# An FFN inside a fused attention block: its steps in twos instead of one by one

## What is computed

```
gate_logits = xf @ Wg + bg
top_w, top_i = jax.lax.top_k(gate_logits, TOP_K)
top_w = jax.nn.softmax(top_w, axis=-1)
w_dense = jnp.sum(jax.nn.one_hot(top_i, E, dtype=xf.dtype) * top_w[..., None], axis=1)
out = jnp.zeros_like(xf)
for e in range(E):
    h = jax.nn.gelu(xf @ W1[e] + b1[e], approximate=False)
    out = out + w_dense[:, e:e + 1] * (h @ W2[e] + b2[e])
```

## Time and profile before

| | |
|---|---|
| time, median of 3 runs | 123.01 us (122.45 to 124.1) |
| time of the profiled execution | 123.65 us |
| its span | 120.6 us |
| mean granted TensorE clock | 0.975 |
| TensorE (PE) busy | 104.9 us |
| VectorE (DVE) busy | 74.1 us |
| ScalarE (ACT) busy | 65.2 us |
| GpSimd (POOL) busy | 20.1 us |

### The profile page before, as it was taken

How to read it: one execution, slowest core, us unless ns; L and a number is a source line. 1 busy time by engine, 2 the same in 40 slices (tenths; PEclk the granted TensorE clock), 3 DMA queues, 4 the chain that set the end, 5 groups by cost and what they waited for, 6 DMA issues and landing times.

```text
span 120.6 us, 2236 instructions
## 1 busy us (share of the span) xinstructions
PE 104.9 (87%) x821; PEld 51.0 (42%) x821; DVE 74.1 (61%) x214; ACT 65.2 (54%) x121; POOL 20.1 (17%) x35
## 2 busy tenths in 40 slices
PE   5946987989899999898999998679999999999930
PEld 2323465664565555465667554551322222222100
DVE  5097379969613559999767689987284224414240
ACT  0405974171788756743539778945536555464600
POOL 7900482000000000000000000000037144124400
PEclk9999999999999999999999999985999999999995
DMA  1910003990000000000000000000000000000003
GB/s 30 230 17 2 0 7 106 228 197 4 0 5 0 0 8 0 0 0 0 5 0 5 0 0 0 0 3 0 0 0 5 0 0 0 0 0 0 0 0 87
DMA packets 6073, 2.83 MB, mean 23 GB/s; under 512 B 4000, under 2 KB 6064, under 8 KB 6064
## 3 DMA queue, kind: packets, MB, share of 16 engines
q1 hardware_dynamic: 5104, 2.19, 9.2%
q10 hardware_dynamic: 960, 0.52, 1.9%
HBM read 2.45 MB, written 0.26 MB: 22 GB/s over the span
## 4 chain that ended last, share of the span: by engine, by line
PE 64%; DVE 17%; ACT 9%; DMA 4%; issue 3%; DVEq 0%
PE bank L913 15%; PE bank L924 13%; PE bank L857 6%; PE bank L790 5%; PE bank L822 4%; DMA x<-in_x_dram 4%; PE bank L871 3%; PE bank L841 3%; PE bank L732 3%; PE bank L741 3%; DVE mx L577 2%; DVE mx L573 2%; ACT sq L393 1%; DVE xn L552 1%; ACT sq L398 1%
## 5 line engine op out<-in xcount | busy, mean ns | idle before, releaser
L472 ACT ACTIVATE hid<-bank,b1c 128x1024 f32<-128x1024 f32 x16 | 17.8, 1115 | 16.9 <-PE bank L913 16.9
L913 PE MATMUL bank<-xn,w_sb 64*128 64x512 f32 x64 | 19.4, 694 | 0.0
L430 ACT ACTIVATE pr<-bank 128x1024 f32<-128x1024 f32 (+1 forms) x16 | 14.0, 914 | 8.5 <-PE bank L828 5.1
L924 PE MATMUL bank<-hid,w_sb 128*64 128x512 f32 x64 | 17.3, 618 | 0.2 <-ACT hid L472 0.2
L692 DVE SCALAR_TENSOR_TENSOR yw<-bank,b2c,wc 128x512 f32<-128x512 f32 x8 | 6.0, 747 | 17.3 <-PE bank L924 17.3
L362 POOL TENSOR_TENSOR acc<-yw,x 64x512 f32<-64x512 f32 x1 | 1.3, 1260 | 70.4 <-DVE yw L692 70.4
L913 PEld LDWEIGHTS bank<-xn,w_sb 64*128 64x128 f32 x64 | 5.3, 196 | 12.4 <-issue 11.6
L708 PE MATMUL bank<-still 128*128 128x512 bf16 (+1 forms) x31 | 8.3, 429 | 2.3 <-DVE still L486 1.3
L367 POOL TENSOR_TENSOR acc<-acc,yw 128x512 f32<-128x512 f32 x6 | 7.6, 1273 | 14.9 <-DVE yw L692 14.9
L573 DVE TENSOR_REDUCE mx<-bank 128x4 f32<-128x1024 f32 x8 | 9.3, 1220 | 1.1 <-PE bank L790 1.0
L790 PE MATMUL bank<-k,q 32*128 32x256 f32 (+1 forms) x128 | 8.3, 373 | 1.3 <-ACT q L418 0.6
(11 more groups left out here) (148 smaller groups left out, 175.5 us busy)
## 6 DMA issues: line engine op xcount, KB each, us to landing
w_sb<-in_L_ffn_W_dram SPq DMA_DIRECT2D x3, 512.0 KB, 7.4
x<-in_x_dram ACTq DMA_DIRECT2D x1, 256.0 KB, 3.9
x<-in_x_dram SPq DMA_DIRECT2D x1, 256.0 KB, 5.0
bqkv<-in_L_attn_b_qkv_dram SPq DMA_DIRECT2D x12, 0.1 KB, 1.5
wo1t<-in_L_attn_W_out_dram SPq DMA_DIRECT2D x8, 4.0 KB, 1.6
out_dram<-acc SPq DMA_DIRECT2D x1, 128.0 KB, 2.5
out_dram<-acc ACTq DMA_DIRECT2D x1, 128.0 KB, 2.9
wq<-in_L_conv_w_qkv_dram ACTq DMA_DIRECT2D x1, 96.0 KB, 4.6
```

Source lines behind the costliest of these rows:

```text
L430: nc.scalar.activation(pr[:, b, 2 * p:2 * p + 2, 0:n], two(key, 0, n), ACT.Exp, scale=SCALE[l]).then_inc(free(key), 1)
L472: nc.scalar.activation(hid[:, k % 3, :, :], two(("h", 0, k)), ACT.Gelu, bias=b1c[:, k:k + 1]).then_inc(free(("h", 0, k)), 1)
L913: i = mm(ps(key, i=s), w1_sb[r, e, P * j:P * j + P], XN[r, 2 * s:2 * s + 2, :].rearrange("p b t -> p (b t)"), start=True, stop=True)
L924: i = mm(ps(key, p0=C * s, p1=C * s + C), w2_sb[:, k, :], hid[:, k % 3, s, :], start=(j == 0), stop=(j == FT - 1))
```

## The change

TensorE does the steps of the FFN in twos: up 2, up 3, down 0, down 1, then up 4, up 5, down 2, down 3, and so on. The first product has three PSUM tiles of two banks (banks 0 to 5) instead of two, the second product two banks (6 and 7) instead of four, and `hid` four places instead of three.

```diff
     for k in range(NK):
-        take(("h", 0, k), 2 * (k % 2), 2)
+        take(("h", 0, k), 2 * (k % 3), 2)
     take(("gate_t", 0), 7)
     for e in range(E):
-        take(("y", 0, e), 4 + e % 4)
+        take(("y", 0, e), 6 + e % 2)
...
-        hid = sb("hid", [P, 3, 2, HALF])
+        hid = sb("hid", [P, 4, 2, HALF])
...
             def gelus(k):
                 filled(act, ("h", 0, k))
-                if k >= 3:
-                    e, j = divmod(k - 3, FT)
+                if k >= 4:
+                    e, j = divmod(k - 4, FT)
                     if j == FT - 1:
                         filled(act, ("y", 0, e))
                     else:
                         act.wait_ge(hused, e + 1)
-                nc.scalar.activation(hid[:, k % 3, :, :], two(("h", 0, k)), ACT.Gelu,
+                nc.scalar.activation(hid[:, k % 4, :, :], two(("h", 0, k)), ACT.Gelu,
...
-                    i = mm(ps(key, p0=C * s, p1=C * s + C), w2_sb[:, k, :], hid[:, k % 3, s, :],
+                    i = mm(ps(key, p0=C * s, p1=C * s + C), w2_sb[:, k, :], hid[:, k % 4, s, :],
...
             up(0)
             up(1)
             pe.wait_ge(ld["w2"], 16)
-            for k in range(NK):
-                if 2 <= k + 1 < NK:
-                    up(k + 1)
-                if k == 1:
+            for e in range(E):
+                if e + 1 < E:
+                    up(FT * e + 2)
+                    up(FT * e + 3)
+                down(FT * e)
+                down(FT * e + 1)
+                if e == 0:
                     key = ("gate_t", 0)
                     claim(pe, key)
                     pe.wait_ge(gsteps, 7)
...
-                down(k)
```

## The result

The changed kernel took 118.91 us (median of 4 runs, 118.48 to 120.73), the kernel before 122.75 us beside it. The ratio is 0.9655, with a 95% interval of 0.9555 to 0.9755, so it is faster by over 2%. The profiled execution took 118.61 us with a span of 116.6. A part of the executions of either kernel shows more time at half clock than others; ratios leave the longest of them out.

The account below looks back on a forecast made before the run. TensorE, busy throughout the FFN, was taken as the bound, losing 0.36 us per pair of changes between `up` and `down`. 2.90 + 0.43 - 0.04 = 3.29 us off 123.01 gave 119.7 us, range 118.9 to 121.2.

Parts of the forecast that it names:

- the one from the FFN to the time: Whole kernel: span 120.6 to 117.3 us, 3.05 outside it kept, profiled 120.36; median 123.01 - 3.29 = 119.7 us.
- 8 pairs of changes at 0.36 = 2.90: FFN on TensorE: 15 runs each of `up` and `down` become 7, saving 8 pairs of changes, 2.90 us.
- The joint: Inside a run, `up` after `up` or `down` after `down`: taken to cost 0, bounds 0 and 0.36 us a pair.
- The last step, 0.43: FFN end: `down(14)` to `down(15)` shrinks from 1.28 to 0.85 us as Gelu 15 comes earlier, 0.43 gained.
- The clock at the start, -0.04: FFN start: `up(2)` streams 0.18 us at half speed, 0.09 lost, 0.05 given back; together -0.04 us.
- Transposes, three tiles, two accumulators: cost 0: FFN: later gate transposes, three first-product tiles with four `hid` places, and two accumulators add no waits; 0 us each.
- The scatter of 0.5 us: Forecast range: runs before lay between 122.45 and 124.1 us, so a median of a few moves by some 0.5.
- (1): Rival, joints inside runs: a joint costs as much as a change, only the tail's 0.43 stays; 122.6 us; chance 0.09.
- (2): Rival, joints: weights aren't loaded beside a matmul on the same rows; 0.45 to 1.33 us less gain; chance 0.09.
- (3): Rival, FFN end: it moves to GpSimd, the spare 0.4 us used up; up to 121.0 us; chance 0.05.
- (4): Rival, FFN periods: a buffer wait for Gelu replaces the changes, 0.3 us in each of seven; 121.8 us; chance 0.03.
- (5): Rival, FFN clock: full grant doesn't return at 83.80, each half-speed `up` or `down` costs 0.85 us more; chance 0.04.

Follow-up runs that it names:

- the two small matmuls: Changed kernel plus a tiny extra matmul per pair, tiled as `up` or otherwise: period 3.89 or 4.10 us against 3.78; one execution each, 120.79 and 122.34 us.
- The tiles alone: Kernel before with three first-product PSUM tiles, two accumulators and four `hid` places, but the old order: 122.83 us, ratio 0.9934, FFN 35.52 us.
- `hid` alone: Kernel before with `hid` at four places and Gelu waits four steps back, nothing else: 123.44 us, ratio 0.9968.
- threes: Changed kernel with `up` and `down` in runs of three instead of two and `hid` at five places: 120.40 us, ratio 0.9759.
- filled gaps: Changed kernel with seven bf16 matmuls of zeros in each of two gaps ahead of the third and fourth gate product: 117.61 us, ratio 0.9549.
- both: Changed kernel with steps in threes and zero matmuls in the gaps ahead of the FFN: 117.26 us, ratio 0.9526, FFN 29.93 us.

## Why the prediction was wrong

Its direction, its mechanism and each term of the sum held. The step that failed is the one from the FFN to the time: "The profiled execution took 123.65 us, 3.05 more than its span, so it would be 120.36", which keeps what lies outside the span as it was, and so "my time is 123.01 - 3.29 = 119.7". The ratio of 0.9655 stands for 118.8 us beside the 123.01 of the runs shown, 0.9 less than forecast and just below the range, which begins at 118.9.

What the runs showed in its place: at equal mean clock the time is 3.9 us shorter and not 3.29, of which 3.4 lie in the span and 0.4 to 0.5 outside it. That makes 119.1 us, inside the range. The other 0.3 is no more than scatter: the interval of the ratio is 117.5 to 120.0 us and holds the forecast, and the three ratios of this kernel, 0.9655, 0.9662 and 0.9737, stand for 118.8, 118.9 and 119.8.

- *8 pairs of changes at 0.36 = 2.90.* The joint costs 0 (loads beside the passes, 0.43 us apart), the period is 3.78 us as forecast, and a change of tiling is what costs (0.21 us between the two small matmuls). Shown.
- *The last step, 0.43.* `down(14)` and `down(15)` are 0.43 us a pass apart without a wait; with its pair of changes 0.77 us from row to row (0.83 by the estimate) for the forecast 0.79. Shown.
- *The clock at the start, -0.04.* In the changed kernel's first profile it fell and rose as before; the FFN gained 3.20 for 3.29.
- *Transposes, three tiles, two accumulators: cost 0.* The tiles alone gave 35.52 us for 35.53. The transposes' copy began at 87.34, the first `yw` at 89.34 and GpSimd kept 0.36 us (0.4 was forecast).
- *Left out: what lies outside the span.* It was taken as unchanged and unaffected by banks. It is 0.50 us less in the mean, and in the old order moving the accumulators alone brings it; why is open, and in the later kernels with these banks it doesn't hold throughout. Nothing in the trace of before shows that they could.
- *Left out: how much the stretch before the FFN varies.* x landed 0.72 us earlier in the profile after, and the clock stands at 0.50 for 3.4 to 6.2 us in the FFN and in some profiles also for 3 us and more early on, from 9 to 11 us. The scatter of 0.5 us that the range allowed for a median was taken from three runs; 11 runs of the kernel before go from 121.80 to 126.88.

3.2 of FFN and 0.5 outside make 3.7, near the 3.84 between the two medians; at equal clock the span gains 3.4, so some 0.2 us of it aren't explained, less than the 0.72 by which x moved between two profiles. Of the rivals, (1) and (2) are refuted by the joints, (3) and (4) by GpSimd's spare time and TensorE's chain without a wait. (5) didn't happen as written, but names the largest thing that was still to be had here: 1.7 us at half clock.

## What to carry to other kernels

Where TensorE is busy all the time, compare the distance from pass to pass with the streaming time: what is missing at a change between two tilings (here 0.15 to 0.21 us each) goes away by putting matmuls of one tiling together, as far as PSUM tiles and buffers reach. Work out how long the engine behind needs for a run, and what the last run waits for; here one more step per run was worth another 0.7 us of the FFN. And look at what stands ahead of a dense stretch: gaps of a microsecond before it cost 1.7 us in it, more than twice what the longer runs gave.

## What the runs showed that I had not expected

- The part of the time outside the span depends on the kernel's banks: 1.93 us and more in 75 executions with the accumulators in banks 4 to 7 (24 of them over 2.5), and in the ten with `hid` alone; 1.66 to 1.76 in 24 with them in banks 6 and 7 and the old order (four of these with `up(15)` moved). It isn't so clean in other kernels with these banks: 1.67 to 2.01 with the change, 1.69 to 2.81 in the six executions of threes, 1.93 to 2.06 with filled gaps, 1.69 to 2.17 with both. The cause stays open.
- The same kernel shows the clock at 0.50 in the FFN for 3.4 us in one execution and 5.7 in another, which is 1.2 us of time; with the gaps filled four executions lie within 0.33 us.
